# Inverse norms of q and k in two attention layers: a power on GpSimd, or Ln and Exp on ScalarE with a Newton step

## The chip, the cores and the metric

The kernel runs on one core of a Trainium2 chip. The metric is the device time of one execution in microseconds, as the median of the runs. Engines are called PE (TensorE), PEld (its weight loads), DVE (VectorE), ACT (ScalarE), POOL (GpSimd) and SP (SyncE), as in the profile.

## The reference

The input is 16 sequences of 512 tokens with 256 channels. A first part, attention over 16 heads with residual and layer norm, is not touched. Then come two layers, and this is what one of them computes for q, k and v:

```python
h = shift_token(x)                      # second half of the channels from the token before
q, k, v = split(h @ wqkv)               # 8 heads of 64
q = l2norm(q) * qs;  k = l2norm(k) * ksc   # l2norm(t) = t / clip(norm(t), 1e-12)
q, k = rotary_xpos(q, k)
o = local_attention(q, k, v)            # windows of 128 keys and the 128 before, softmax
x = x + o @ wo
h = layernorm(shift_token(x)) * lg + lb
a, g = split(h @ w1 + b1)
x = x + (a * gelu(g)) @ w2 + b2
```

After both layers a residual and a final layer norm are added. All inputs and outputs are float32.

## The kernel before, in words

The first part (`head_attention`) runs first, up to about 1560 us. The rest is `layers`. It works through 32 sequences (16 in layer 1, numbered 0 to 15, and the same 16 in layer 2, numbered 16 to 31), each in 4 tiles of 128 tokens. `T` is the tile's number, `w_` its place in its sequence (0 to 3). Every engine has its own list of instructions, which it carries out strictly in the order written; `one(n, par, r, layer)` writes the four tiles of sequence n. The first four, the last two of layer 1, the first two of layer 2 and the last ones are written out singly, the others run in hardware loops. Engines wait for one another on semaphores.

The work is staggered. While tile T is in attention, the engines project q, k and v of tile T+1, and the feed-forward part works on tile T-4: its hidden values come in three chunks (i = 0, 1, 2) in `hidden` (L1445), ScalarE adds the bias to the gate half of each (`gate`, L1056) and VectorE to the value half (`value`, L1196). `value` waits for `gate` of its chunk. When the gate values of half a sequence (two tiles) are there, ScalarE applies Gelu to all of them in two instructions (L1109, L1110); this is done in the tiles with w_ = 0 and w_ = 2, for sequences n-2 and n-1. VectorE multiplies the value half of the first of the two tiles by it (`gated`, L843 and L845), GpSimd the second. Then PE forms the product with w2 (L1524), which waits for `gated`.

The norms: ScalarE squares q and k of tile T+1 out of PSUM (`squares`), VectorE sums them per head into `ss` (L1163) and clips them into `ssc` (L1167, 128 x 16), GpSimd raises `ssc` to the power -0.5 (`norms`, L959) into `rn`. `rn` is read by `scale_k` on VectorE (L1171), after which PE transposes k (L1474), and in the next tile by the exp bias (L1187) and the exps (L1137).

Within one tile the orders that matter are these. ScalarE: layer norm of T-2, q and k evacuated, gate(T,0), evacuate_hT, oT, exps of half 0, squares(T+1), PT evacuated, Gelu where there is one, gate(T,1), exps of half 1, evacuate_v(T+1), gate(T,2), PT evacuated. VectorE: ..., row_max of half 0, the residual x2, final_stats (in layer 2, w_ = 0 and 2), rot_products(T+1) with ss and ssc, value(T,1), row_max of half 1 (L1184) with the exp bias (L1187), gated, value(T,2), scale_k(T+1), final_norm, layer-norm statistics of T-1, residual xo. GpSimd: rounding rest of hnT, rotate(T+1), norms(T+1), the final rstd (L995), rstd (L1000), its half of gated. PE: ..., hidden(T,1), scores of half 1, times_v, v of T+1, hidden(T,2), the w2 product, transposes of the probabilities of half 1, and then the next tile's transposes of q and k.

Each function of ScalarE needs a table that holds it. [...] Where the program doesn't name a set, the load (ACT_TABLE_LOAD) is put directly in front of the first instruction that needs another one; it carries the line of that instruction.

Of the kernel before, what the change touches and what calls it, by code (L numbers as in the profile page):

```python
# [47 lines left out]
def head_attention(nc, ctx, x_in, w, x_out, consts, W0=None, raw=None):  # L48
# [6 lines left out]


    ident, identr, half = consts["ident"], consts["identr"], consts["minus_half"]
    ones_row, minus_identb = consts["ones_row"], consts["minus_identb"]

    def sb(name, shape, dtype=F32):  # L60
        return ctx.enter_context(nc.sbuf_tensor("a_" + name, shape, dtype))
# [542 lines left out]
def make_constants(nc, ctx):  # L604
    def sb(name, shape, dtype=F32):
        return ctx.enter_context(nc.sbuf_tensor("c_" + name, shape, dtype))

    c = {"ident": sb("ident", [P, P]), "identr": sb("identr", [P, P], F32R),
         "identb": sb("identb", [P, P], BF16), "minus_identb": sb("minus_identb", [P, P], BF16),
         "minus_half": sb("half", [P, 16]), "ones_row": sb("ones", [1, P])}  # L610
    s_i = ctx.enter_context(nc.semaphore("c_identity"))
    with nc.Block() as block:
        @block.gpsimd
        def _(pool):
            nc.gpsimd.memset(c["minus_half"][:], -0.5).then_inc(s_i, 1)
            nc.gpsimd.memset(c["ones_row"][:], 1.0).then_inc(s_i, 1)
            nc.gpsimd.memset(c["ident"][:], 0.0).then_inc(s_i, 1)
            pool.wait_ge(s_i, 3)
            nc.gpsimd.affine_select(out=c["ident"][:], in_=c["ident"][:], compare_op=ALU.not_equal, fill=1.0, base=0,
                                    pattern=[[-1, P]], channel_multiplier=1).then_inc(s_i, 1)  # L620

        @block.vector
        def _(dve):
            dve.wait_ge(s_i, 4)
            nc.vector.tensor_copy(c["identr"][:], c["ident"][:]).then_inc(s_i, 1)
            nc.vector.tensor_copy(c["identb"][:], c["ident"][:]).then_inc(s_i, 1)
            nc.vector.tensor_scalar(c["minus_identb"][:], c["ident"][:], -1.0, None, ALU.mult).then_inc(s_i, 1)
            dve.wait_ge(s_i, 7)
    return c


# [54 lines left out]
def layers(nc, ctx, x_a, x_b, y_out, w, W, raw, consts):  # L686
# [37 lines left out]
    t2 = [sb(f"t2{i}", [P, LHEADS, LDIM]) for i in range(2)]  # L724
    ss = sb("ss", [P, 2 * LHEADS])
    ssc = sb("ssc", [P, 2 * LHEADS])
    rn = [sb(f"rn{i}", [P, 2 * LHEADS]) for i in range(2)]
    qT = sb("qT", [P, 2, PAIRS, P], F32R)
    kT = sb("kT", [P, 2, PAIRS, 2, P], F32R)
# [43 lines left out]
    s_ss = sem("sums_of_squares")  # L773
    s_qr = sem("q_rotated")
    s_ks = sem("k_sum")
    s_rn = sem("norms")
    s_kr = sem("k_rotated")
    s_qkT = sem("qkT")
# [169 lines left out]
    def _(pool):  # L948
# [5 lines left out]
            nc.gpsimd.tensor_tensor(t1[1][:], t1[1][:], t2[1][:], ALU.add).then_inc(s_ks, 1)  # L954

        def norms(t, p):
            pool.wait_ge(s_ss, 2 * t + 2)
            need(pool, s_pr, 2 * t - 2)
            nc.gpsimd.tensor_tensor(rn[p][:], ssc[:], half[:], ALU.pow).then_inc(s_rn, 1)  # L959

        nc.gpsimd.memset(zero_col[:], 0.0).then_inc(s_c, 1)
        for i in range(2):
            nc.gpsimd.memset(hT1[i][:].bitcast(F32), 0.0).then_inc(s_c, 1)
            nc.gpsimd.memset(a_sb[i][:], 1.0).then_inc(s_c, 1)
            nc.gpsimd.memset(mask[i][:], 0.0).then_inc(s_c, 1)
        nc.gpsimd.memset(hs[:], 0.0).then_inc(s_c, 1)
        pool.wait_ge(s_c, 8)
        for i in range(2):

            nc.gpsimd.affine_select(out=mask[i][:, i], in_=mask[i][:, i], compare_op=ALU.is_ge, fill=MASKED, base=0,  # L970
# [39 lines left out]
    def _(act):  # L1010
# [28 lines left out]
        def squares(t):  # L1039
# [3 lines left out]
            act.wait_ge(s_k, t + 1)  # L1043
            nc.scalar.activation(sq[:, 1], X[1][:], ACT.Square).then_inc(s_sq, 1)

        def evacuate_v(t, w_):
            act.wait_ge(s_v, t + 1)
            need(act, s_AV, t - 2)
            nc.scalar.activation(v[:, w_], X[2][:], ACT.Copy).then_inc(s_ve, 1)
# [18 lines left out]

        split_high(0)
        act.wait_ge(s_w, WEIGHTS)  # L1070
        act.wait_ge(s_c, 12)
        evacuate_hT(-1, -1, 3, lambda d: 0)
        squares(0)
        evacuate_v(0, 0)

        def one(n, par, r, layer):
            for w_ in range(TILES):
                T = TILES * n + w_
                p = w_ % 2
                live, feed = tile_exists(T), seq_exists(n - 1)  # L1080
                if tile_exists(T - 2):
                    layernorm(T - 2, p, (w_ - 2) % TILES, par if w_ >= 2 else 1 - par)
                if live:
                    act.wait_ge(s_qkT, 2 * T + 1)
                    nc.scalar.activation(qT[:, HIGH], X[0][:].rearrange("p (b q) -> p b q", q=P), ACT.Copy).then_inc(s_qkTe, 1)
                    act.wait_ge(s_qkT, 2 * T + 2)
                    nc.scalar.activation(kT[:, HIGH, :, p], X[1][:].rearrange("p (b q) -> p b q", q=P), ACT.Copy
                                         ).then_inc(s_qkTe, 1)
                if feed:
                    gate(T, 0, w_, layer)  # L1090
                if tile_exists(T + 1) or tile_exists(T - 2):
                    evacuate_hT(T, n, w_, layer)
                if tile_exists(T - 1):
                    act.wait_ge(s_oT, T)
                    nc.scalar.activation(oT[:], M[:], ACT.Copy).then_inc(s_oTe, 1)
                if live:
                    exps(T, w_, 0)
                if tile_exists(T + 1):
                    squares(T + 1)
                if live:  # L1100
                    act.wait_ge(s_PT, 2 * T + 1)
                    evacuate_PT(w_, 0)
                if w_ % 2 == 0:
                    h, d = (1, 2) if w_ == 0 else (0, 1)
                    m = n - d
                    if seq_exists(m):

                        act.wait_ge(s_Fg, 3 * (TILES * m + 2 * h + 2))
                        nc.scalar.activation(g_sb[h][0:HC, 0:CHUNKS - 1], g_sb[h][0:HC, 0:CHUNKS - 1], ACT.Gelu)  # L1109
                        nc.scalar.activation(g_sb[h][0:LAST, CHUNKS - 1], g_sb[h][0:LAST, CHUNKS - 1], ACT.Gelu  # L1110
                                             ).then_inc(s_ge, 1)
                if feed:
                    gate(T, 1, w_, layer)
                if live:
                    exps(T, w_, 1)
                if tile_exists(T + 1):
                    evacuate_v(T + 1, (w_ + 1) % TILES)
                if feed:
                    gate(T, 2, w_, layer)
                if live:  # L1120
                    act.wait_ge(s_PT, 2 * T + 2)
                    evacuate_PT(w_, 1)
                if split_at(n, w_) is not None:
                    split_high(split_at(n, w_))
                if isinstance(n, int) and n == ALL_SEQS + 1 and w_ == 2:
                    break
# [22 lines left out]
    def _(dve):  # L1149
        def rot_products(t, w_, layer):  # L1150
# [13 lines left out]
                                    ).then_inc(s_ss, 1)  # L1164
            dve.wait_ge(s_ss, 2 * t + 1)
            need(dve, s_rn, t)
            nc.vector.tensor_scalar(ssc[:], ss[:], 1e-24, None, ALU.max).then_inc(s_ss, 1)  # L1167

        def scale_k(t, p):
            dve.wait_ge(s_rn, t + 1)  # L1170
# [40 lines left out]
            nc.vector.tensor_tensor(hT1[1 - p][:, LOW, 0:1], last_col, hT1[1 - p][:, HIGH, 0:1], ALU.subtract  # L1211
                                    ).then_inc(s_hTl, 1)

        dve.wait_ge(s_c, 12)
        split_low(0)
        low_hT(-1, 3)
        dve.wait_ge(s_w, WEIGHTS)
# [116 lines left out]
    def _(pe):  # L1334
# [114 lines left out]
            last.then_inc(s_F, 1)  # L1449

        pe.wait_ge(s_w, WEIGHTS)
        pe.wait_ge(s_c, 12)
        tile_parity["next"] = 0
        transpose_h(-1, -1, 3, 1)
        projection_ready(0, 0)
# [145 lines left out]
```

## Time and profile before

| | |
|---|---|
| time, median of 3 runs | 4568.05 us (4567.26 to 4568.8) |
| the profiled execution | 4568.7 us, its span 4566.8 us |
| mean granted TensorE clock | 0.982 |
| busy: PE, PEld | 4268.7 us (93%), 3555.8 us (78%) |
| busy: DVE, ACT, POOL | 3151.7 us (69%), 2677.8 us (59%), 2373.7 us (52%) |

Times are microseconds unless marked ns. In the rows of stretches the engines stand in the order PE, PEld, DVE, ACT, POOL, with the number of instructions in brackets. A busy share is one of the engine's whole span. "Idle before" is the time in which an engine stood still ahead of an instruction, with the instruction that ended it behind the arrow. Ends of matmuls are modelled, so a product can seem to overlap the next by 0.1 to 0.2 us.

### The profile page before, as it was taken

What the parts mean: (1) busy time and instruction counts of PE and PEld (TensorE: products, weight loads), DVE (VectorE), ACT (ScalarE), POOL (GpSimd) and SP (SyncE); (2) the same over time, 40 slices, a digit from 0 to 9 for tenths busy, and PEclk for the clock granted to TensorE, in tenths of its full rate; (3) what the DMA queues carried; (4) which work ended last, traced back from release to release, by engine and by line L of the source; (5) the groups of instructions that cost most, each with busy time, mean ns of one, the idle gap of its engine ahead of it and who ended that gap; (6) DMA issues with size and microseconds to landing.
All of it is one profiled execution on the core that took longest, in us unless ns stands there. A gap on an engine that the chain in (4) does not pass through costs nothing.

```text
span 4566.8 us, 99388 instructions
## 1 busy us (share of the span) xinstructions
PE 4268.7 (93%) x36868; PEld 3555.8 (78%) x36928; DVE 3151.7 (69%) x5876; ACT 2677.8 (59%) x6240; POOL 2373.7 (52%) x1655
## 2 busy tenths in 40 slices
PE   5999999999999589999999999999999999999998
PEld 3666666666676478888888888888888888888887
DVE  4989898898999655565555555555666666666664
ACT  3544454444544256666766666666666666666664
POOL 4989898898999633333333333333333333333332
PEclk8999999999999899999999999999999999999999
DMA  5443444344443100000000000000000000000000
GB/s 107 68 61 58 64 68 69 60 60 65 67 64 50 44 27 13 13 16 18 16 14 17 20 14 15 18 28 13 20 21 25 18 23 18 26 20 20 21 21 25
DMA packets 175117, 160.11 MB, mean 35 GB/s; under 512 B 22175, under 2 KB 173558, under 8 KB 174582
## 3 DMA queue, kind: packets, MB, share of 16 engines
q1 hardware_dynamic: 174582, 153.04, 18.1%
q8 instruction: 329, 5.39, 0.5%
q14 instruction: 206, 1.69, 0.1%
HBM read 52.31 MB, written 25.17 MB: 17 GB/s over the span
## 4 chain that ended last, share of the span: by engine, by line
PE 46%; DVE 7%; issue 6%; ACT 4%; POOL 2%; SPq 0%; DVEq 0%; DMA 0%; ACTq 0%; POOLq 0%
PE b_X L1374 10%; PE b_F L1445 7%; PE b_M L1419 7%; PE b_M L1497 5%; PE b_F L1524 5%; PE b_S L1399 4%; PE b_S L1408 3%; PE b_M L1488 2%; PE b_S L1390 2%; ACT b_p L1137 1%; PE b_X L1470 1%; PE b_X L1474 1%; POOL b_rn L959 1%; ACT b_hn L1036 1%; DVE b_ss L1163 1%
## 5 line engine op out<-in xcount | busy, mean ns | idle before, releaser
L321 ACT ACTIVATE a_p<-a_S 128x512 f32<-128x512 f32 x1024 | 529.3, 603 | 593.4 <-PE a_S L507 593.4
L373 DVE TENSOR_REDUCE a_nm<-a_S 128x128 fp32r<-128x2048 f32 x256 | 586.3, 2290 | 130.2 <-PE a_S L497 123.6
L1137 ACT ACTIVATE b_p<-b_S,b_nb,b_rn 128x256 f32<-128x256 f32 (+1 forms) x1024 | 536.7, 534 | 230.5 <-DVE b_nb L1187 229.7
L1374 PE MATMUL b_X<-b_wqkv,b_hT 128*128 128x512 f32 x2304 | 648.2, 417 | 3.6 <-DVE b_hT L1211 1.3
L250 POOL TENSOR_TENSOR a_z<-a_p 128x1024 f32<-128x1024 f32 x256 | 604.0, 2360 | 74.4 <-ACT a_p L321 73.1
L1445 PE MATMUL b_F<-b_hnT,b_w 128*114 128x256 f32 (+1 forms) x4608 | 630.6, 286 | 5.7 <-issue 5.7
L1445 PEld LDWEIGHTS b_F<-b_hnT,b_w 128*114 128x114 f32 (+1 forms) x4608 | 575.3, 178 | 18.6 <-issue 5.9
L952 POOL TENSOR_TENSOR b_t<-b_t 128x512 f32<-128x512 f32 x128 | 165.6, 1293 | 792.3 <-DVE b_t L1161 792.3
L1374 PEld LDWEIGHTS b_X<-b_wqkv,b_hT 128*128 128x128 f32 x2304 | 417.3, 190 | 91.4 <-issue 8.0
L1196 DVE TENSOR_SCALAR b_a<-b_F,w_b 114x256 f32<-114x256 f32 (+1 forms) x384 | 183.8, 479 | 432.3 <-ACT b_g L1056 432.1
L258 POOL TENSOR_TENSOR a_p<-a_p,a_zi 128x640 f32<-128x640 f32 x256 | 397.4, 1552 | 98.9 <-DVE a_zi L399 98.5
L1419 PE MATMUL b_M<-b_v,b_PT 128*128 128x64 f32 x3584 | 445.4, 276 | 0.0
L1419 PEld LDWEIGHTS b_M<-b_v,b_PT 128*128 128x128 f32 x3584 | 424.3, 193 | 15.0
L1143 ACT ACTIVATE b_PT<-b_S 128x1024 f32<-128x1024 f32 (+1 forms) x256 | 235.2, 919 | 319.6 <-PE b_S L1408 319.6
L401 DVE TENSOR_TENSOR a_p<-a_p,a_O 128x1408 f32<-128x1408 f32 x256 | 412.2, 1610 | 0.0
L507 PE MATMUL a_S<-a_nm,c_identr 128*128 128x512 f32 x1024 | 313.8, 428 | 95.8 <-DVE a_nm L373 85.1
L959 POOL TENSOR_TENSOR b_rn<-b_ssc,c_half 128x16 f32<-128x16 f32 x128 | 372.7, 2912 | 21.2 <-DVE b_ssc L1167 16.8
L984 POOL TENSOR_TENSOR b_hnT<-b_hnT 128x256 fp32r<-128x256 f32 x128 | 93.8, 733 | 555.5 <-ACT b_hnT L1027 555.5
L507 PEld LDWEIGHTS a_S<-a_nm,c_identr 128*128 128x128 f32 x1024 | 175.0, 191 | 266.1 <-DVE a_nm L373 229.4
L1524 PE MATMUL b_F<-w_w,b_a 114*128 114x256 f32 (+1 forms) x1536 | 361.9, 385 | 15.8 <-DVE b_a L845 14.4
L1000 POOL TENSOR_TENSOR b_rstd<-b_ve,c_half 128x1 f32<-128x1 f32 x128 | 71.0, 555 | 562.7 <-DVE b_ve L1288 562.7
L253 POOL TENSOR_TENSOR a_z<-a_z 128x512 f32<-128x512 f32 x256 | 327.8, 1280 | 23.0 <-POOL a_z L250 5.7
(143 smaller groups left out, 8805.4 us busy)
## 6 DMA issues: line engine op xcount, KB each, us to landing
a_q<-a_parts SPq DMA_DIRECT2D x256, 128.0 KB, 4.9
a_k<-a_parts SPq DMA_DIRECT2D x256, 128.0 KB, 5.0
a_x<-in_x SPq DMA_DIRECT2D x16, 512.0 KB, 4.1
a_xr<-in_x SPq DMA_DIRECT2D x64, 128.0 KB, 5.0
x_after_heads<-a_n SPq DMA_DIRECT2D x64, 128.0 KB, 5.0
b_x<-x_after_heads SPq DMA_DIRECT2D x16, 512.0 KB, 3.9
x_after_layer<-b_xo SPq DMA_DIRECT2D x32, 256.0 KB, 2.2
b_x<-x_after_layer SPq DMA_DIRECT2D x16, 512.0 KB, 3.9
```

The lines of the kernel that those rows point to most:

```text
L250: nc.gpsimd.tensor_tensor(z8[:], e[:, 0:8], e[:, 8:16], ALU.add).then_inc(s_zt, 1)
L258: nc.gpsimd.tensor_tensor(e, e, zinv[u % 2][:].unsqueeze(1).to_broadcast([P, HEADS - DVE_HEADS, P]), ALU.mult).then_inc(s_pp, 1)
L321: nc.scalar.activation(probs[u % NE][:, hs], S[:, hs], ACT.Exp, scale=HDIM ** -0.5).then_inc(s_exp, 1)
L373: nc.vector.tensor_reduce(out=negmax[u % 2][:], in_=S[:].rearrange("p h q -> p q h"), axis=AX.X, op=ALU.max, negate=True).then_inc(s_nm, 1)
L401: nc.vector.tensor_tensor(e, e, ZI.unsqueeze(1).to_broadcast([P, DVE_HEADS, P]), ALU.mult).then_inc(s_p, 1)
L507: nc.tensor.matmul(S[:, 4 * b:4 * b + 4], identr[:], negmax[u % 2][:].unsqueeze(1).to_broadcast([P, 4, P]), start=False, stop=True, skip_g ...
L959: nc.gpsimd.tensor_tensor(rn[p][:], ssc[:], half[:], ALU.pow).then_inc(s_rn, 1)
L1137: last = nc.scalar.activation(probs[hf][:, i, keys(w_)], SB[:, i, keys(w_)], ACT.Exp, bias=nb[hf][:, i:i + 1], scale=rn[w_ % 2][:, h:h + 1 ...
L1374: last = nc.tensor.matmul(X[i][:], hT_of(k, a), wqkv[:, b, k, i * INNER:(i + 1) * INNER], start=(k == 0 and (a, b) == PART_PAIRS[0]), stop ...
L1419: last = nc.tensor.matmul(M[:, h * LDIM:(h + 1) * LDIM], PT[hf][:, i, a * P:(a + 1) * P], v[:, w_ if a == w_ % 2 else w_ - 1, h * LDIM:(h ...
L1445: last = nc.tensor.matmul(F[i % 2][0:size, part], w1[:, a, k, col:col + size], hnT[:, b, k, hf * 2 * P:(hf + 1) * 2 * P], start=(k == 0 an ...
L1524: last = nc.tensor.matmul(F[1][:, t], a_sb[h][0:rows, c, t * P:(t + 1) * P], W[layer(-d)]["w2"][0:rows, c], start=(c == 0), stop=(c == CHU ...
```

## The change

GpSimd's power is replaced by a first estimate from ScalarE, exp(-0.5 ln(ss)), and one Newton step g(1.5 - 0.5 ss g g) in four GpSimd instructions. For that `ssc` now holds -0.5 times the clipped sums. The table set that has both Ln and Exp is named in the program: once before the first tile, and after every pair of Gelus. `guess_norms(T+1)` stands between gate(T,1) and exps of half 1. An unused row of ones is dropped, and the counts of a few waits change with the constants.

```diff
@@ layers
+    ln_ss, guess = sb("ln_ss", [P, 2 * LHEADS]), sb("guess", [P, 2 * LHEADS])
+    newton, three_halves = sb("newton", [P, 2 * LHEADS]), sb("three_halves", [P, 2 * LHEADS])
...
@@ gpsimd
         def norms(t, p):
-            pool.wait_ge(s_ss, 2 * t + 2)
+            pool.wait_ge(s_gs, t + 1)
+            nc.gpsimd.tensor_tensor(newton[:], guess[:], guess[:], ALU.mult).then_inc(s_nw, 1)
+            pool.wait_ge(s_nw, 3 * t + 1)
+            nc.gpsimd.tensor_tensor(newton[:], newton[:], ssc[:], ALU.mult).then_inc(s_nw, 1)
+            pool.wait_ge(s_nw, 3 * t + 2)
+            nc.gpsimd.tensor_tensor(newton[:], newton[:], three_halves[:], ALU.add).then_inc(s_nw, 1)
+            pool.wait_ge(s_nw, 3 * t + 3)
             need(pool, s_pr, 2 * t - 2)
-            nc.gpsimd.tensor_tensor(rn[p][:], ssc[:], half[:], ALU.pow).then_inc(s_rn, 1)
+            nc.gpsimd.tensor_tensor(rn[p][:], newton[:], guess[:], ALU.mult).then_inc(s_rn, 1)
...
+        nc.gpsimd.memset(three_halves[:], 1.5).then_inc(s_c, 1)
@@ scalar
+        def guess_norms(t):
+            act.wait_ge(s_ss, 2 * t + 2)
+            nc.scalar.activation(ln_ss[:], ssc[:], ACT.Ln, scale=-2.0).then_inc(s_ls, 1)
+            act.wait_ge(s_ls, t + 1)
+            need(act, s_rn, t)
+            nc.scalar.activation(guess[:], ln_ss[:], ACT.Exp, scale=-0.5).then_inc(s_gs, 1)
...
         squares(0)
+        nc.scalar.preload_act_table_set("natural_log_exp_and_others")
+        guess_norms(0)
         evacuate_v(0, 0)
...
                         nc.scalar.activation(g_sb[h][0:LAST, CHUNKS - 1], g_sb[h][0:LAST, CHUNKS - 1], ACT.Gelu
                                              ).then_inc(s_ge, 1)
+                        nc.scalar.preload_act_table_set("natural_log_exp_and_others")
                 if feed:
                     gate(T, 1, w_, layer)
+                if tile_exists(T + 1):
+                    guess_norms(T + 1)
                 if live:
                     exps(T, w_, 1)
@@ vector
-            nc.vector.tensor_scalar(ssc[:], ss[:], 1e-24, None, ALU.max).then_inc(s_ss, 1)
+            nc.vector.tensor_scalar(ssc[:], ss[:], 1e-24, -0.5, ALU.max, ALU.mult).then_inc(s_ss, 1)
```

## Rows read from the trace of the kernel before

**Rows 1.** busy time by stretch (start:end, length, engines, PEclk, DMA share, GB/s)

```profile
1900.00:2100.00 200.00, 199.09 (x1441) 175.43 (x1440) 119.86 (x288) 137.98 (x340) 70.81 (x55) 1.00 0.05 16
3300.00:3500.00 200.00, 193.78 (x1381) 169.76 (x1379) 122.51 (x313) 131.37 (x330) 65.52 (x54) 0.99 0.07 20
```

**Rows 2.** the page, chain that ended last, by line, share of span

```profile
PE b_X L1374 10%; PE b_F L1445 7%; PE b_M L1419 7%; PE b_M L1497 5%; PE b_F L1524 5%; PE b_S L1399 4%; PE b_S L1408 3%; PE b_M L1488 2%; PE b_S L1390 2%; ACT b_p L1137 1%; PE b_X L1470 1%; PE b_X L1474 1%; POOL b_rn L959 1%; ACT b_hn L1036 1%; DVE b_ss L1163 1%
```

**Rows 3.** lines L959 (ns) and L1171 (waited for: us, times)

```profile
L959 POOL TENSOR_TENSOR b_rn<-b_ssc,c_half x128: 2909/2912/2919, 1588.8 to 4477.6; 128x16 f32<-128x16 f32 x128
...
  POOL b_rn L959: 9.6, 5
```

**Rows 4.** timeline of ScalarE, layer 1, w_ = 0 (start, length)

```profile
2040.82 0.40 ACT L1110 ACTIVATE b_g<-b_g 112x256 f32<-112x256 f32 x1
2041.13 0.46 ACT L1056 ACTIVATE b_g<-b_F,w_b 114x256 f32<-114x256 f32 x1
2041.60 1.28 ACT L1137 ACT_TABLE_LOAD   x1
2042.93 0.46 ACT L1137 ACTIVATE b_p<-b_S,b_nb,b_rn 128x128 f32<-128x128 f32 x1
```

**Rows 5.** timeline of VectorE, the same tile

```profile
2041.62 0.48 DVE L1196 TENSOR_SCALAR b_a<-b_F,w_b 114x256 f32<-114x256 f32 x1 [0.99 <-ACT b_g L1056]
2042.02 0.68 DVE L1184 TENSOR_REDUCE b_mx<-b_S 128x4 f32<-128x512 f32 x1
2042.73 0.16 DVE L1187 SCALAR_TENSOR_TENSOR b_nb<-b_mx,b_rn 128x4 f32<-128x4 f32 x1
2042.93 0.83 DVE L843 TENSOR_TENSOR b_a<-b_a,b_g 114x640 f32<-114x640 f32 x1
2043.68 0.28 DVE L845 TENSOR_TENSOR b_a<-b_a,b_g 112x128 f32<-112x128 f32 x1
```

**Rows 6.** timeline of PE, the same tile

```profile
2044.09 2.85 PE L1524 MATMUL b_F<-w_w,b_a 114*128 114x256 f32 x12
```

**Rows 7.** timelines of three other kinds of gelu tile

```profile
1999.44 0.28 DVE L845 TENSOR_TENSOR b_a<-b_a,b_g 112x128 f32<-112x128 f32 x1
...
1999.87 2.85 PE L1524 MATMUL b_F<-w_w,b_a 114*128 114x256 f32 x12
...
2899.42 0.28 DVE L845 TENSOR_TENSOR b_a<-b_a,b_g 112x128 f32<-112x128 f32 x1
...
2900.00 2.76 PE L1524 MATMUL b_F<-w_w,b_a 114*128 114x256 f32 x12
...
3315.44 0.46 ACT L1056 ACTIVATE b_g<-b_F,w_b 114x256 f32<-114x256 f32 x1
...
3316.44 0.47 DVE L1196 TENSOR_SCALAR b_a<-b_F,w_b 114x256 f32<-114x256 f32 x1
...
3318.49 0.28 DVE L845 TENSOR_TENSOR b_a<-b_a,b_g 112x128 f32<-112x128 f32 x1
...
3318.90 2.85 PE L1524 MATMUL b_F<-w_w,b_a 114*128 114x256 f32 x12 [0.58 <-DVE b_a L845]
```

**Rows 8.** line L1137, its table loads (ns)

```profile
L1137 ACT ACT_TABLE_LOAD  x61: 1283/1283/1283, 1729.5 to 4477.9; - x61
```

**Rows 9.** timeline of ScalarE: a one-column Copy; exps, ordinary tile

```profile
2007.08 0.19 ACT L1020 ACTIVATE b_hT<-b_X 128x1 fp32r<-128x1 f32 x1
...
2019.68 0.56 ACT L1137 ACTIVATE b_p<-b_S,b_nb,b_rn 128x256 f32<-128x256 f32 x1 [2.36 <-DVE b_nb L1187]
```

**Rows 10.** timeline of GpSimd: 256 and 512 columns

```profile
2008.75 0.73 POOL L984 TENSOR_TENSOR b_hnT<-b_hnT 128x256 fp32r<-128x256 f32 x1 [2.40 <-ACT b_hnT L1027]
...
2016.61 1.27 POOL L954 TENSOR_TENSOR b_t<-b_t 128x512 f32<-128x512 f32 x1
```

**Rows 11.** timelines of VectorE and PE, the drain

```profile
4534.75 1.62 DVE L845 TENSOR_TENSOR b_a<-b_a,b_g 112x128 f32<-112x128 f32 x1
...
4536.43 4.55 PE L1524 MATMUL b_F<-w_w,b_a 114*128 114x256 f32 x12 [2.78 <-DVE b_a L845]
```

More of the change, by code:

```diff
@@ L57, in head_attention @@
     ident, identr, half = consts["ident"], consts["identr"], consts["minus_half"]
-    ones_row, minus_identb = consts["ones_row"], consts["minus_identb"]
+    minus_identb = consts["minus_identb"]
     def sb(name, shape, dtype=F32):
@@ L609, in make_constants @@
          "identb": sb("identb", [P, P], BF16), "minus_identb": sb("minus_identb", [P, P], BF16),
-         "minus_half": sb("half", [P, 16]), "ones_row": sb("ones", [1, P])}
+         "minus_half": sb("half", [P, 16])}
     s_i = ctx.enter_context(nc.semaphore("c_identity"))
@@ L615, in _ @@
             nc.gpsimd.memset(c["minus_half"][:], -0.5).then_inc(s_i, 1)
-            nc.gpsimd.memset(c["ones_row"][:], 1.0).then_inc(s_i, 1)
             nc.gpsimd.memset(c["ident"][:], 0.0).then_inc(s_i, 1)
-            pool.wait_ge(s_i, 3)
+            pool.wait_ge(s_i, 2)
             nc.gpsimd.affine_select(out=c["ident"][:], in_=c["ident"][:], compare_op=ALU.not_equal, fill=1.0, base=0,
@@ L623, in _ @@
         def _(dve):
-            dve.wait_ge(s_i, 4)
+            dve.wait_ge(s_i, 3)
             nc.vector.tensor_copy(c["identr"][:], c["ident"][:]).then_inc(s_i, 1)
@@ L627, in _ @@
             nc.vector.tensor_scalar(c["minus_identb"][:], c["ident"][:], -1.0, None, ALU.mult).then_inc(s_i, 1)
-            dve.wait_ge(s_i, 7)
+            dve.wait_ge(s_i, 6)
     return c
@@ L775, in layers @@
     s_ks = sem("k_sum")
+    s_ls = sem("ln_squares")
+    s_gs = sem("norms_guessed")
+    s_nw = sem("newton_step")
     s_rn = sem("norms")
@@ L966, in _ @@
         nc.gpsimd.memset(hs[:], 0.0).then_inc(s_c, 1)
-        pool.wait_ge(s_c, 8)
+        pool.wait_ge(s_c, 9)
         for i in range(2):
@@ L1070, in _ @@
         act.wait_ge(s_w, WEIGHTS)
-        act.wait_ge(s_c, 12)
+        act.wait_ge(s_c, 13)
         evacuate_hT(-1, -1, 3, lambda d: 0)
         squares(0)
+        nc.scalar.preload_act_table_set("natural_log_exp_and_others")
+        guess_norms(0)
         evacuate_v(0, 0)
@@ L1212, in low_hT @@
                                     ).then_inc(s_hTl, 1)
-        dve.wait_ge(s_c, 12)
+        dve.wait_ge(s_c, 13)
         split_low(0)
@@ L1451, in _ @@
         pe.wait_ge(s_w, WEIGHTS)
-        pe.wait_ge(s_c, 12)
+        pe.wait_ge(s_c, 13)
         tile_parity["next"] = 0
```

## The prediction

> **What bounds the kernel now.** I read the busy time by stretch first (is there an engine with no room?), then the chain and the waits around the power (does anyone wait for the norms?), and last the timelines of single tiles (what comes level with PE?).
>
> The change touches only the layers, after about 1590 us. There PE works 199.09 of 200 us in layer 1 and 193.78 of 200 in layer 2, POOL about 70 [rows 1]. So time that PE loses is lost for good, and time that GpSimd saves counts only where PE waits for it.
>
> It hardly does. The chain gives the power (L959) 1% [rows 2], but the instruction that reads the norms, the scaling of k (L1171), sat idle for them 5 times in 128 tiles, 9.6 us in all [rows 3]. Elsewhere the norms are there before anyone asks. The shares of the chain are inferred; the idle time is what I go by.
>
> What does bind is found in the tiles with a gelu (T with w_ = 0 or 2). There ScalarE does: table load, two Gelus, gate(T,1) (L1056), table load, exps. In the tile shown the Gelus end at 2040.82+0.40 = 2041.22, the gate starts at 2041.13 (back-to-back operations overlap by 0.09), and only then comes the load for Exp, 1.28 us, ending at 2042.88 [rows 4]. VectorE waits for that gate and starts value(T,1) 0.03 us after it; behind it in its queue stand row_max, the exp bias, and gated, whose last part ends at 2043.96 [rows 5]. PE starts the w2 product at 2044.09, 0.13 us later [rows 6]. Where PE is seen to stand idle for L845, the product also starts 0.13 us after it (3318.77 to 3318.90, rows 7), so 0.13 is the latency of that wait and the slack here is nil. The chain gate, value, row_max, bias, gated, w2 product is thus already level with PE, in a stage where PE has no room.
>
> **The change part by part.**
>
> 1. *The table load moves ahead of the gate.* The number of loads in live tiles doesn't change: one before the Gelus, one after. Before, the second stood behind gate(T,1) and in front of exps, where ScalarE would have waited for the bias anyway: load and bias end within 0.01 us of each other, at 2042.88 and 2042.89 [rows 4, 5]. Now it is issued right behind the second Gelu, ahead of the gate. The gate then starts at 2041.22 + 1.28 + 0.01 = 2042.51 instead of 2041.13: 1.38 us later. Queued behind it: value(T,1), row_max, bias and gated on VectorE, and with them the w2 product; exps, evacuate_v and gate(T,2) on ScalarE, value(T,2), scale_k and the layer-norm statistics after those. All move by about the same amount, so PE stalls once per such tile and finds the others no later than itself. There are 61 such tiles, as many as loads in front of Exp [rows 8]: sequences 1 to 31 with w_ = 2, sequences 2 to 31 with w_ = 0. By kind (layer 2's final_stats runs from sequence 18 on):
>  - layer 1, w_ = 0, 16 tiles, slack nil: 16 x 1.38 = 22.1 us.
>  - layer 1, w_ = 2, 17 tiles. L845 ends at 1999.72 and the product starts at 1999.87: 0.15, less the latency 0.13, leaves 0.02 to 0.06 in the 10 looped ones. In the 7 written out singly the distance is 0.30 (2899.70 to 2900.00, rows 7); I take 0.25 of it as slack. 10 x 1.35 + 7 x 1.13 = 21.4.
>  - layer 2, w_ = 2, 14 tiles (12 looped): 12 x 1.35 + 2 x 1.13 = 18.5.
>  - layer 2, w_ = 0, 14 tiles: final_stats holds VectorE, value(T,1) starts at 3316.44 though the gate ended at 3315.44 + 0.46 = 3315.90 [rows 7], so 0.5 us of the delay is covered (I take 0.4 in two of them): 12 x 0.88 + 2 x 0.98 = 12.5.
>  Sum: 74.5 us. Nothing hides it, because the wait that it lengthens is PE's.
>
> The Trainium skill (ScalarE: Activation LUTs, "What ACT_TABLE_LOAD costs") has every switch at 1283 ns for the load and some 1380 ns of drain. The load's length agrees with rows 8 (1283 ns); the drain does not show in rows 4, where the exps start 0.05 us after the load. By the page's sum the gate would be 2.8 us late in each of the 61 tiles: that is rival E.
>
> 2. *Ln and Exp on ScalarE* (guess_norms, between gate(T,1) and exps). No row shows them at 128x16. A Copy of 128x1 takes 0.19 us [rows 9], which is the lower end; an Exp of 128x128 takes 0.46 [rows 4], the upper. I take 0.20, the nearest in columns, with 0.1 for the two waits: 0.5 us for both, 1.1 at most. They wait for ssc, which VectorE writes before value(T,1), row_max and the bias that exps wait for. From the gate's end to the exps are 0.03+0.40+0.68+0.03+0.16+0.04 = 1.34 us even in the short tile [rows 4, 5]; in an ordinary tile ScalarE idles 2.36 us there [rows 9]. Cost nothing; without that cover, 0.5 us for each of 128 tiles.
>
> 3. *GpSimd: four small products and sums for one power.* Removed: 2.91 us a tile [rows 3]. Added: 128x256 takes 0.73 and 128x512 1.27 us [rows 10], so 2.1 ns a column and 0.22 us at 16 columns. With a wait of 0.1 each, 4 x 0.32 = 1.3 us; at most 4 x 0.73 + 0.4 = 3.3, at least 0.9. Guess and step together take 1.8 where the power took 2.9. Behind them in the queue are frstd, rstd and gated's half, none of which had waited for the power. In ordinary tiles the norms come earlier and nobody takes them earlier: 0. In a gelu tile they start 0.5 us after a gate that is itself late: 2042.97 + 0.5 + 1.3 = 2044.8, before even the delayed gated ends (2043.96 + 1.38); scale_k stands behind that and value(T,2), so the norms are still early. Gain: only where L1171 waited. The first power starts at 1588.8 [rows 3] and PE has nothing else to do then, gain about 1.1. The four others sit where PE waits for exps anyway: 0.1 each. Together -1.5 us.
>
> 4. *GpSimd and VectorE side by side.* In the tiles with w_ = 0 the last small GpSimd operation may fall on gated (L843, 0.83 us beside the power, rows 5). The nearest row of two such operations together is the L845 of 1.62 us instead of 0.28 in the drain [rows 11]. The bounds are 0 and +1.34 for each of 30 tiles (+40); the power next to L843 cost nothing and a 16-column operation is short, so I take 0 and keep +10 in the range.
>
> 5. *ssc with a second operator, the new constants, the missing ones row.* Same instruction, same size; memsets before the stage starts: 0, at most 1 us once.
>
> 6. *The drain.* Sequence 32 has no exps, so there no second load stood before; now each Gelu has one behind it, and the next Gelu needs its own. At (32, w_ = 2) that is two loads, 2.57 us, ahead of the gate; final_stats on VectorE covers an estimated 0.3 of it, and PE idles behind L845 already, 2.78 us [rows 11]: +2.3. The others hide behind PE or final_stats. Bounds 0 and +5.
>
> Sum: 74.5 - 1.5 + 2.3 = +75.3 on the profiled execution's 4568.7 us (span 4566.8): 4644.0. The median of the runs is 0.65 below it: **4643 us**, 1.6% slower.
>
> **The rivals.**
>
> *A: the load is hidden after all.* If the load ahead of the gate were placed where Exp is (or PE had room I don't see), the w2 products stay where they are and only part 3's gain is left: 4568.05 - 1.5 = 4567. For it: the loads of before stand directly ahead of their function. Against: rows 4 to 7 leave 0 to 0.25 us of room for 1.38.
>
> *B: the norms matter more than the waits say; faster.* If the chain's 1% were true, the power's 46 us are on the path, and 1.1 of each 2.9 us goes: -17 us. With A's hiding this ends at 4568 - 17 = 4551, faster. It decides if L1171's idle time is misread. Against it: rows 3. With the gate's delay it would be 4626, which is within the range.
>
> *C: the set that serves both isn't kept.* If Ln and Exp each called their own set, an ordinary tile would get two more loads, 2.57 us, plus 0.4, in a gap of 2.36 (+0.6 for 67 tiles) and a gelu tile at least one more before exps (+0.8 to 1.3 for 61): 4643 + 40 + 65 = 4748. The Trainium skill (same page, "Table sets: the hidden batching unit") says that one set holds both, so one load serves them; no row of before shows it.
>
> *D: half of it comes back.* PE idles 6.2 us of 200 in layer 2 [rows 1]; if the shift fed itself into those idle places, up to 0.6 us of each of the 28 tiles there would return: 4643 - 17 = 4626.
>
> *E: ScalarE stands still behind a load.* If another 1.38 us went by before the gate, it would be 61 x 1.38 = 84 us more: 4727. Against it: 0.05 us from load to exps in rows 4, with a bias that ended in the same moment. It is the skill's drain (the section named in part 1).
>
> **How the numbers follow.** Forecast 0.77, D 0.07, A 0.05, B 0.03 (faster only in its pure form), C 0.04, E 0.02, something lost beyond the range 0.02. This kernel's runs tell 0.2% (9 us) from no change. Slower: 0.77+0.07+0.04+0.02+0.02 = 0.92; same 0.05; faster 0.03. The range takes in D and B with the gate's delay below, less a few us for gelu tiles that have more room than those shown, and above it the contention of part 4 and 5 us of drain: 4612 to 4664.
>
> **What would show it.** In the changed profile: L1056 behind a Gelu starts 1.29 us after the Gelu's end, with a load between; the w2 product gets an idle time <- L845 of 0.9 to 1.4 us in some 61 tiles, some 75 us in all (before there are few such waits); PE's busy time stays; the load counts stay near 64 and 64. Ln and Exp at 0.2 us each, with exps still released by the bias; L1171 no longer waits for rn beyond the first tiles; GpSimd's busy time falls by 128 x (2.9-0.9) = 260 us with no gain. I am wrong if the w2 product waits no longer than before, if loads turn up in ordinary tiles, or if exps wait for GpSimd or for Ln.

## The result, and the profile after

| | before | after |
|---|---|---|
| time, median of 4 runs side by side | 4568.43 us (4567.26 to 4577.63) | 4663.48 us (4656.82 to 4670.61) |
| the profiled execution: time, span | 4568.7, 4566.8 us | 4658.6, 4656.8 us |
| mean granted TensorE clock | 0.982 | 0.983 |

The change makes the kernel slower: ratio 1.0206, 95% interval 1.0194 to 1.0218, about 94 us. The forecast was 4643 us with a range of 4612 to 4664. The measured median lies 0.5 us inside the upper end of that range. The two profiled executions are 90.0 us apart in span; the accounting below is made of these.

The page's line of busy times, of the changed kernel (us, share of the span, instructions):

```profile
PE 4287.7 (92%) x36928; PEld 3557.0 (76%) x36928; DVE 3154.2 (68%) x5876; ACT 2744.3 (59%) x6502; POOL 2131.3 (46%) x2039
```

GpSimd has 242 us less to do and the kernel is 90 us longer. What PE waited for in the layers, first after, then before (us in total, times, longest):

```profile
PE b_F L1547 <- DVE b_a L849: 88.6, 64, 3.9
PE b_X L1379 <- ACT b_hn L1047: 29.8, 33, 6.5
```

```profile
PE b_X L1356 <- ACT b_hn L1036: 24.8, 38, 6.5
...
PE b_F L1524 <- DVE b_a L845: 14.4, 17, 3.5
```

One line moved much: the w2 product (L1547, before L1524) waits for `gated` 64 times instead of 17, and 88.6 us instead of 14.4: +74.2 us. The same tile as [rows 4 to 6], on ScalarE, VectorE, GpSimd and PE of the changed kernel (start, length; the last bracket is idle time and its releaser):

```profile
2054.06 0.40 ACT L1130 ACTIVATE b_g<-b_g 112x256 f32<-112x256 f32 x1
2054.48 1.28 ACT L1132 ACT_TABLE_LOAD   x1
2055.78 0.47 ACT L1074 ACTIVATE b_g<-b_F,w_b 114x256 f32<-114x256 f32 x1
2056.15 0.21 ACT L1059 ACTIVATE b_ln_ss<-b_ssc 128x16 f32<-128x16 f32 x1
2056.39 0.22 ACT L1062 ACTIVATE b_guess<-b_ln_ss 128x16 f32<-128x16 f32 x1
2057.60 0.46 ACT L1160 ACTIVATE b_p<-b_S,b_nb,b_rn 128x128 f32<-128x128 f32 x1 [0.99 <-DVE b_nb L1210]
```

```profile
2056.28 0.48 DVE L1219 TENSOR_SCALAR b_a<-b_F,w_b 114x256 f32<-114x256 f32 x1 [2.43 <-ACT b_g L1074]
2056.68 0.68 DVE L1207 TENSOR_REDUCE b_mx<-b_S 128x4 f32<-128x512 f32 x1
2057.40 0.16 DVE L1210 SCALAR_TENSOR_TENSOR b_nb<-b_mx,b_rn 128x4 f32<-128x4 f32 x1
2057.60 0.83 DVE L847 TENSOR_TENSOR b_a<-b_a,b_g 114x640 f32<-114x640 f32 x1
2058.34 0.31 DVE L849 TENSOR_TENSOR b_a<-b_a,b_g 112x128 f32<-112x128 f32 x1
```

```profile
2056.68 0.21 POOL L962 TENSOR_TENSOR b_newton<-b_guess 128x16 f32<-128x16 f32 x1 [2.86 <-ACT b_guess L1062]
...
2057.28 0.22 POOL L966 TENSOR_TENSOR b_newton<-b_newton,b_three_halves 128x16 f32<-128x16 f32 x1
2057.65 0.85 POOL L969 TENSOR_TENSOR b_rn<-b_newton,b_guess 128x16 f32<-128x16 f32 x1 [0.16 <-POOL b_newton L966]
```

```profile
2055.70 1.56 PE L1468 MATMUL b_F<-b_hnT,b_w 128*114 128x256 f32 x12
2058.78 2.86 PE L1547 MATMUL b_F<-w_w,b_a 114*128 114x256 f32 x12 [1.51 <-DVE b_a L849]
```

Read them as a relay. The second Gelu ends at 2054.46, the load takes ScalarE to 2055.76, and the gate starts at 2055.78 where it stood 0.09 us ahead of the Gelu's end before. `value` follows the gate's start by 0.50 us (before 0.49), the product follows `value` by 2.50 us (before 2.47): every leg has its old length, and the baton is late by the load alone. PE ended its other work at 2057.26 and stands for 1.51 us. Behind the gate ScalarE has 0.99 us to spare before its exps, so Ln and Exp cost nothing there.

### The profile page after: what moved, and what is told of

Its sections match the earlier page's. It is cut to its first block, busy times and chain, and to the rows that moved or that the text cites. A ratio compares the mean times of both kernels' runs of the same rounds, so it can differ in the third digit from the quotient of the medians.

```text
span 4656.8 us, 100507 instructions
## 1 busy us (share of the span) xinstructions
PE 4287.7 (92%) x36928; PEld 3557.0 (76%) x36928; DVE 3154.2 (68%) x5876; ACT 2744.3 (59%) x6502; POOL 2131.3 (46%) x2039
## 3 DMA queue, kind: packets, MB, share of 16 engines
q14 instruction: 213, 1.74, 0.1%
## 4 chain that ended last, share of the span: by engine, by line
PE 36%; issue 14%; ACT 7%; DVE 4%; POOL 4%; POOLq 0%; SPq 0%; DMA 0%; DVEq 0%; ACTq 0%
PE b_X L1397 8%; PE b_M L1442 5%; PE b_F L1468 5%; PE b_M L1520 4%; PE b_F L1547 4%; PE b_S L1431 3%; PE b_S L1422 3%; PE b_M L1511 1%; ACT L1129 1%; ACT L1132 1%; PE b_S L1413 1%; ACT b_p L1160 1%; DVE b_mx L1207 1%; ACT b_g L1074 1%; POOL b_t L956 1%
## 5 line engine op out<-in xcount | busy, mean ns | idle before, releaser
L1547 PE MATMUL b_F<-w_w,b_a 114*128 114x256 f32 (+1 forms) x1536 | 363.6, 386 | 89.2 <-DVE b_a L849 88.6
L1547 PEld LDWEIGHTS b_F<-w_w,b_a 114*128 114x128 f32 (+1 forms) x1536 | 284.6, 192 | 138.0 <-issue 71.3
```

The costliest lines, as they stand in the source:

```text
L1547: last = nc.tensor.matmul(F[1][:, t], a_sb[h][0:rows, c, t * P:(t + 1) * P], W[layer(-d)]["w2"][0:rows, c], start=(c == 0), stop=(c == CHU ...
```

## The experiments

Ratios are to the kernel before, run on the same chip in the same series, with a 95% interval. "Step" is by how much a w2 product falls further behind the same product of the kernel before, in the profiles; all steps together give the difference of the spans.

**1. The load alone, without the new norms** (before_load_ahead).

```diff
 (kernel before, behind the second Gelu)
+                        nc.scalar.preload_act_table_set("exp_and_others")
```

> The kernel before, power and all, with one addition: the load of Exp's table is named right behind the second Gelu, so that it runs ahead of gate(T,1). Theory L: it loses what the change lost in these tiles, 16 x 1.45 + 31 x 1.35 + 14 x 0.96 = 78.5 us and some 2 in the drain: 4568 + 80 = 4648, range 4640 to 4660. Rival N: 4568, since no norm is touched. Rival H: the layers start at 1561.8 as before, because no constant is touched; if they start late here too, it is the run and not the kernel.

Measured: 4652.8 us, ratio 1.0186 (1.0169 to 1.0203). PE's wait for `gated`:

```profile
PE b_F L1525 <- DVE b_a L845: 88.0, 64, 3.9
```

With power where it was, and this one line of the change, the 88 us are there. The steps by kind of tile are those of the changed kernel (layer 1, w_ = 0: 1.43; w_ = 2 looped 1.40, written singly 1.18; layer 2, w_ = 0: 0.93 us; in the changed kernel 1.45, 1.40, 1.18 and 0.95).

**2. The changed kernel with its load behind the gate** (load_behind_gate).

```diff
 (kernel after)
-                        nc.scalar.preload_act_table_set("natural_log_exp_and_others")
                 if feed:
                     gate(T, 1, w_, layer)
+                if w_ % 2 == 0 and seq_exists(n - (2 if w_ == 0 else 1)):
+                    nc.scalar.preload_act_table_set("natural_log_exp_and_others")
```

> The changed kernel, with the table load after the Gelus put back behind gate(T,1), ahead of Ln. Theory L (the load ahead of the gate is the whole loss, 61 tiles of about 1.4 us): the w2 product waits for gated as rarely as before, and the kernel comes back to about 4577 us where before is 4568: 2 us of drain, and some 9 us because in the 30 tiles with w_ = 0 load, Ln and Exp end 0.45 us after the exp bias, so that gate(T,2) and the layer norm of the tile come that much later. Range 4566 to 4584. Rival N (Ln, Exp and the four GpSimd operations cost the time by themselves): it stays above 4620. Rival H (part of the loss, about 4 us, comes from the constants that moved, since the attention part ended 4.1 us later in the changed kernel's profile): the first instruction of the layers on ScalarE starts at 1565.9 here too, not at 1561.8.

Measured: 4591.66 us, ratio 1.0057 (1.004 to 1.0073). The wait for `gated` is gone, but the kernel stays 21 us behind that of before, above the range I had written. What stands where (PE's wait for `gated`; then ScalarE at the load; then ScalarE and PE at the back-edge of layer 1's loop):

```profile
PE b_F L1548 <- DVE b_a L849: 15.2, 17, 3.6
```

```profile
2045.54 1.28 ACT L1135 ACT_TABLE_LOAD   x1
2046.83 0.22 ACT L1059 ACTIVATE b_ln_ss<-b_ssc 128x16 f32<-128x16 f32 x1
2047.08 0.22 ACT L1062 ACTIVATE b_guess<-b_ln_ss 128x16 f32<-128x16 f32 x1
2047.21 0.44 ACT L1161 ACTIVATE b_p<-b_S,b_nb,b_rn 128x128 f32<-128x128 f32 x1
```

```profile
2123.04 0.49 ACT L1047 ACTIVATE b_hn<-b_x,b_shift,b_rstd 128x128 f32<-128x128 f32 x1 [1.89 <-DVE b_shift L1258]
2125.09 0.49 ACT L1047 ACTIVATE b_hn<-b_hs,b_shift,b_rstd 128x128 f32<-128x128 f32 x1 [1.56 <-issue]
```

```profile
2125.63 0.44 PE L1380 MATMUL b_X<-c_ident,b_hn 128*128 128x128 f32 x2 [1.96 <-ACT b_hn L1047]
2125.91 3.21 PE L1443 MATMUL b_M<-b_v,b_PT 128*128 128x64 f32 x16
```

Two smaller costs come to light. One had been hidden by the load ahead of the gate. In this order Ln and Exp stand between the load, which ends level with the bias, and the exps, which start 0.38 us later for it: 0.28 us a step in layer 1's first tiles (w_ = 0), 16 x 0.28 = 4.5 us. The other is in the changed kernel too (part 2 below): at each of the four back-edges of layer 1's loop ScalarE stands 1.6 to 1.8 us for nothing that the trace names, between the two hn instructions. In the one shown PE then waits 1.96 us, and after that its 16 small matmuls take 3.21 us, where they take 1.90 at the full clock. The granted clock in these stretches was (window, length, busy times by engine, PEclk):

```profile
2123.00:2126.00 3.00, 1.04 (x10) 0.80 (x8) 0.00 (x0) 1.41 (x4) 0.00 (x0) 1.00 0.02 8
2126.00:2129.00 3.00, 3.00 (x18) 3.00 (x17) 1.68 (x3) 2.70 (x10) 0.22 (x1) 0.54 0.00 0
```

The four back-edges gave steps of 4.38, 1.74, 4.66 and 1.84 us, 12.6 together. The two large ones are those where the small matmuls slowed down (3.21 and 3.19 us), after waits of PE of 1.96 and 2.46 us; after waits of 1.99 and 2.30 us at the two others they kept 1.90. With the 4.5 these make 17 of the 21 us. Of the rest, 3.0 us stood before the first gelu tile (2.7 of them before the layers, see below) and 1.1 in the drain.

**3. Norms that cost next to nothing** (cheap_norms). The power is replaced by a subtraction, so rn is no inverse norm.

```diff
 (kernel before)
-            nc.gpsimd.tensor_tensor(rn[p][:], ssc[:], half[:], ALU.pow).then_inc(s_rn, 1)
+            nc.gpsimd.tensor_tensor(rn[p][:], ssc[:], half[:], ALU.subtract).then_inc(s_rn, 1)
```

> The kernel before with GpSimd's power replaced by one subtraction of the same shape, so that rn holds no inverse norm (that part of the computation is left out): 0.22 us instead of 2.91 in every tile. It is the most that any cheaper norm can bring. Theory L (nobody waits for the norms but the first tiles): 4566 us where before is 4568, -3 to 0. Rival B (the chain's 1% for the power is real): -17 to -46 us, 4522 to 4551.

Measured: 4567.24 us, ratio 0.9995 (0.9985 to 1.0004). GpSimd's busy time fell from 2373.7 to 2028.1 us for nothing. VectorE's wait for the norms, which was 9.6 us in 5 times [rows 3]:

```profile
DVE b_t L1171 <- POOL b_rn L959: 0.3, 1, 0.3
```

So the whole cost of the power was below 0.2%. Rival B, by which the norms lie on the path, falls.

**4. Two loads ahead of the gate** (two_loads_ahead).

```diff
 (kernel after, behind the second Gelu)
+                        nc.scalar.preload_act_table_set("exp_and_others")
                         nc.scalar.preload_act_table_set("natural_log_exp_and_others")
```

> The changed kernel with a second table load (Exp's own set, then the set of both) ahead of gate(T,1). Theory L: each microsecond ahead of the gate is paid 61 times, now without slack: +61 x 1.28 = 78 us above the changed kernel, and 1 to 3 in the drain: ratio to before 1.037 to 1.040, about 4742 us if the changed kernel is at 4663. Rival: if part of the loss in the changed kernel is not the gate's delay but something that a second load doesn't add to (norms, code, constants), it is still +78 for this step, but load_behind_gate then stays well above before; if the two loads run beside each other or with a standstill of 1.38 us each, the step is near 0 or near 160.

Measured: 4806.18 us, ratio 1.053 (1.0513 to 1.0548); span 146.9 us above the changed kernel's. I expected +78. PE's wait for `gated` and its busy time:

```profile
PE b_F L1548 <- DVE b_a L849: 169.0, 64, 5.2
```

```profile
PE 4363.9 (91%) x36868; PEld 3631.4 (76%) x36928; DVE 3154.5 (66%) x5876; ACT 2822.4 (59%) x6566; POOL 2130.6 (44%) x2039
```

I had written that a standstill with each load would bring the step near 160, and 147 is not far from that. But the two loads follow each other without one:

```profile
1967.54 1.28 ACT L1132 ACT_TABLE_LOAD   x1
1968.83 1.28 ACT L1133 ACT_TABLE_LOAD   x1
1970.12 0.47 ACT L1074 ACTIVATE b_g<-b_F,w_b 114x256 f32<-114x256 f32 x1
```

The wait grew by 80.4 us, 78.5 of it in the 61 tiles, as the theory has it, and 1.9 in the drain, which has three more such loads. But PE was also busy for 76.2 us longer with the same matmuls. The products of two gelu tiles, and the granted clock behind the second (window, its length, the five engines' busy times, and then PEclk):

```profile
1926.15 2.86 PE L1548 MATMUL b_F<-w_w,b_a 114*128 114x256 f32 x12 [2.31 <-DVE b_a L849]
...
1973.15 4.54 PE L1548 MATMUL b_F<-w_w,b_a 114*128 114x256 f32 x12 [2.83 <-DVE b_a L849]
```

```profile
1973.00:1975.00 2.00, 1.85 (x5) 1.56 (x6) 0.32 (x2) 1.66 (x6) 0.00 (x0) 0.63 0.00 0
1975.00:1978.00 3.00, 3.00 (x13) 2.42 (x13) 1.71 (x8) 0.00 (x0) 1.23 (x2) 0.68 0.01 3
1978.00:1980.00 2.00, 2.00 (x20) 2.00 (x18) 0.37 (x2) 1.83 (x5) 1.25 (x2) 1.00 0.01 4
```

After standing 2.83 us PE ran at a lower granted clock, 0.63 over the next 2 us (a mean of the 2.4 and the 1.2 GHz level), and the product took 4.54 us instead of 2.86. After 2.31 us in the tile shown it did not, and after the changed kernel's 1.51 us neither. Over the 61 tiles, all 22 products behind a stand of 2.79 us or more took 3.98 us or more; of the 39 behind 2.29 to 2.62 us, 27 were slow and 12 kept 2.85 or 2.86. A second load thus costs nearly twice its length (146.9 us for 61 tiles). The stands of ScalarE at layer 1's back-edges are absent in this kernel, though it has Ln and Exp.

**5. The gate of chunk 1 ahead of the Gelus, in the kernel before** (gate_first) **and after** (gate_first_after). This was to be the better version.

```diff
+                if feed:
+                    gate(T, 1, w_, layer)
                 if w_ % 2 == 0:
                     h, d = (1, 2) if w_ == 0 else (0, 1)
...
-                if feed:
-                    gate(T, 1, w_, layer)
```

> The kernel before, with ScalarE's gate of chunk 1 moved ahead of the Gelu block instead of behind it. Theory (what ends last at a Gelu tile is the path gate, VectorE's value and product, down-projection on TensorE): the path gets shorter by the Gelu block, so the 14.4 us that TensorE waits for the gated product (17 times in layers' loops) go, and some of the 24.8 us that it waits for ScalarE's hn; against that the Gelu itself is later by one gate (0.3 to 0.5 us) at its own reader, which is not near. Ratio 0.994 to 0.998 (about -10 to -25 us). Rival (the product of the chunk before, or the maxima of VectorE, end the wait just as late): ratio 0.999 to 1.001.

> The changed kernel with the same move: ScalarE's gate of chunk 1 stands ahead of the Gelu block and so ahead of the load that was put behind the Gelu. Theory (the 88.6 us of waits for the gated product are the load of 1.28 us in the gate's path and nothing else): the waits go back to below 15 us, and the ratio to the kernel before is 0.996 to 1.004. Rival (the load costs by standing ahead of the second half's exponentials, or the norms' new chain costs): the ratio stays above 1.01.

Measured: 4591.67 us, ratio 1.0044 (1.0027 to 1.0061), and 4625.94 us, ratio 1.0125 (1.0106 to 1.0143). In the kernel before the move loses 20 us instead of gaining 10 to 25. The waits of PE and, below, ScalarE in a gelu tile of gate_first:

```profile
PE b_X L1356 <- ACT b_hn L1036: 34.3, 45, 6.5
...
PE b_F L1524 <- DVE b_a L845: 17.1, 17, 3.5
PE b_X L1474 <- DVE b_t L1171: 8.5, 19, 4.5
```

```profile
2045.86 0.47 ACT L1056 ACTIVATE b_g<-b_F,w_b 114x256 f32<-114x256 f32 x1 [0.76 <-PE b_F L1445]
2046.35 1.28 ACT L1111 ACT_TABLE_LOAD   x1
```

The 14.4 us that PE waited for `gated` did not hang on the gate, and they are still there: 14 of the 17 waits are the w_ = 0 tiles of layer 2 (0.24 to 0.59 us each), where `value` starts behind final_stats [rows 7], and three are in the drain. In the looped w_ = 0 tiles of layer 1 the move does bring the w2 product 0.2 to 0.5 us sooner, but the next product then falls back by 1.1. What the move did is make ScalarE wait for the hidden product (0.76 us here) before the Gelus instead of doing the Gelus meanwhile, so that Gelu, load, exps and all behind them came later: in this tile PE then stood 0.18 us for the scaled k, 0.51 for hn and 0.24 for o_n, where before only the last was there. In gate_first_after the wait for `gated` is

```profile
PE b_F L1547 <- DVE b_a L849: 18.5, 17, 4.4
```

so 70 of the 88.6 us went by taking the load off the gate's path, as in experiment 2, and the wait for hn rose to 51.4 us in their place. My upper figure for this run (1.004) was missed. The profile has two things for it: the product behind each w_ = 0 tile of layer 1 falls back by 1.2 to 1.5 us (0.9 to 1.1 in gate_first), and ScalarE stands 1.5 us at the four back-edges of layer 1, which in gate_first it does not; the steps there are 5.65, 1.28, 1.21 and 1.34 us.

**6. Two small operations on ScalarE, without and with Ln's wait** (two_more_copies, waiting_copies).

```diff
 (kernel before, behind gate(T, 1); the two tiles `spare` are new)
+                if tile_exists(T + 1):
+                    act.wait_ge(s_ss, 2 * (T + 1) + 2)     # waiting_copies alone
+                    need(act, s_rn, T + 1)                 # waiting_copies alone
+                    for i in range(2):
+                        nc.scalar.activation(spare[i][:], half[:], ACT.Copy)
```

> The kernel before, with two copies of 128x16 on ScalarE into tiles that nobody reads, in each tile with a successor, where the changed kernel has its Ln and Exp; power, and the loads where they were. Theory (the two operations as such are hidden, and the 1.6 us for which ScalarE stands between the two hn instructions at the loop's back-edges of layer 1 comes from the number of its instructions in the loop's body): +0 to +10 us, ratio 1.000 to 1.002, and the stand between the two hn instructions is in the trace, 4 times. Rival (the stand has to do with the Ln and Exp's waits or with where the load stands): ratio 0.999 to 1.001 and no such stand.

> The kernel before, with the two copies of 128x16 on ScalarE of the kernel two_more_copies (they read a constant and write tiles that nobody reads), and ahead of them the waits that the changed kernel has ahead of its Ln: for VectorE's clamped sums of the next tile, and for GpSimd's norm of this one; power, and the loads where they were. Theory (the stand of 1.6 us between the two hn instructions at the back-edges of layer 1, and the 0.28 us of a first tile, both come with this wait standing in ScalarE's order ahead of the second half's exponentials): the stand is in the trace 4 times, and the ratio is 1.002 to 1.005, near the kernel with the load behind the gate. Rival (they come with Ln and Exp themselves, or with where the load stands): no stand, ratio 0.999 to 1.001.

Measured: ratio 1.0004 (0.9994 to 1.0014) and 1.0043 (1.0027 to 1.006). The two operations as such are nearly hidden: no stand at the back-edges, steps of 0.12 to 0.20 in the w_ = 0 tiles of layer 1, 2.6 us together. So the number of instructions alone was not the cause of the stand. With the waits, the ratio rises to near that of experiment 2, with steps of 0.12 to 0.21 in the w_ = 0 tiles of layer 1, 0.4 to 0.5 in those of layer 2, and 0.62 to 1.14 at the four back-edges of layer 1. There ScalarE stands again, but at another place and for half as long:

```profile
2124.69 0.60 ACT L1088 ACTIVATE b_kT<-b_X 128x512 fp32r<-128x512 f32 x1 [0.73 <-issue]
```

The theory is right in a small part: waits in that place bring a stand at the back-edge, but not the 1.6 us one between the hn instructions, and they add nothing to the steps of the w_ = 0 tiles of layer 1. The ratio fell into the range that I had written by luck: the steps of 0.4 to 0.5 in layer 2 make some 6 us of it, and experiment 2 has none there.

**7. Ln and Exp behind the exps** (norms_after_exps), in the kernel of experiment 2.

```diff
-                if tile_exists(T + 1):
-                    guess_norms(T + 1)
                 if live:
                     exps(T, w_, 1)
                 if tile_exists(T + 1):
+                    guess_norms(T + 1)
                     evacuate_v(T + 1, (w_ + 1) % TILES)
```

> The changed kernel with its load behind the gate of chunk 1, and Ln and Exp of the next tile behind the second half's exponentials instead of ahead of them. Theory (what is left of the cost once the load is off the gate's path is the wait of Ln for the clamped sums, ahead of the exponentials): the 0.28 us of each first tile goes, with or without the stand at the back-edges, and the ratio to the kernel before is 0.999 to 1.003, below that of the load behind the gate (1.0057). Rival (the norms are then late for k's rotation and the transposes behind it, since Ln, Exp and four Newton steps of 0.3 us start 2 us later): ratio above 1.005, with longer waits of TensorE for VectorE's scaled k than 4.8 us.

Measured: 4626.39 us, ratio 1.0122 (1.0105 to 1.0139). The range that I had written for the theory was missed, and the 0.28 us did not go: the steps behind the w_ = 0 tiles of layer 1 are 0.31 to 0.43. The rival was right in direction, but only for the start: the norms come late in the first five tiles, before 1681 us, and nowhere else, and the first w2 product is 9.1 us late. VectorE's wait for the norms, and PE's for the scaled k and for hn:

```profile
DVE b_t L1195 <- POOL b_rn L969: 16.9, 5, 3.9
```

```profile
PE b_X L1380 <- ACT b_hn L1047: 43.3, 40, 5.7
...
PE b_X L1498 <- DVE b_t L1195: 9.0, 7, 4.0
```

The back-edges of layer 1 cost 4.5 to 6.1 us each here, 23 us of the 60 by which the spans differ. In layer 2 the products fall back by 0.3 to 0.5 us for every gelu tile, 12 us together; why, was not tested. Of the orders tried for the new norms, that of experiment 2 is the cheapest, and none reaches the kernel before.

## Why the prediction was right, point by point

The direction, the mechanism and its place were as forecast; the total was 15 us (profiled) to 20 us (medians) too low. That the median still lies in the range, by 0.5 us, is in part luck: the room above the forecast was meant for contention and for the drain, and neither used it. It was used up by larger steps, by the stands at the back-edges, by a later start of the layers, and by differences between single executions. Against the 90.0 us of the two spans:

| term | forecast | measured |
|---|---|---|
| 1. load ahead of the gate | 74.5 | 78.5 by steps, 74.2 by PE's waits |
| 2. Ln and Exp | 0 | 0 in this order; back-edges of layer 1: +6.4 |
| 3. norms earlier | -1.5 | -1.0 |
| 4. GpSimd beside VectorE | 0 | 0 |
| 5. constants, start of the layers | 0, at most 1 | +1.9 |
| 6. drain | +2.3 | +1.3 |
| the part before the layers (unchanged) | 0 | +4.1 |
| tiles ahead of the first Gelu | 0 | -1.2 |

*Part 1.* By kind of tile the steps were 1.45, 1.40 (1.18 where written singly), 1.40 (1.18) and 0.95 (1.06 to 1.13) us; forecast were 1.38, 1.35 (1.13), 1.35 (1.13) and 0.88 (0.98). All are larger by some 0.06 us, which over 61 tiles is near 4 us: the gate used to overlap the Gelu by 0.09 and now follows the load after 0.02 (I had 1.38 for 1.28 + 0.09 + 0.01), and the legs behind it are 0.01 to 0.03 longer. Experiments 1 and 2 show this term from both sides: the load alone brings it, the load behind the gate takes it away. Rivals A and D fall with it. The steps of the w_ = 0 tiles at the five back-edges of layer 2 scatter (1.17, -0.01, 2.15, 0.22 and 0.07 us), as they do in other profiles (-1.93 to 1.80 in experiment 2); together they are 1.2 us below five plain ones, which is all that layer 2 can have given back.

*Part 2.* Ln and Exp take 0.21 and 0.22 us; I had 0.20. They cost nothing where they stand, but for a reason that the change itself makes: with the load ahead of the gate, ScalarE is idle between gate and exps. That cover was forecast at 1.34 us and measured 1.35 (2056.25 to 2057.60 above). It holds for this order alone: with the load in its old place it fills the gap, and the steps are 0.28 us in the w_ = 0 tiles. What I missed is the stand at the loop's back-edges of layer 1: steps of 2.89, 3.12, 3.04 and 3.24 us where a plain tile has 1.45, 4 x 1.6 = 6.4 us. The rows, with the same instruction of before behind them (there no stand):

```profile
2134.72 0.49 ACT L1047 ACTIVATE b_hn<-b_x,b_shift,b_rstd 128x128 f32<-128x128 f32 x1 [1.80 <-DVE b_shift L1257]
2136.85 0.49 ACT L1047 ACTIVATE b_hn<-b_hs,b_shift,b_rstd 128x128 f32<-128x128 f32 x1 [1.63 <-issue]
```

```profile
2118.88 0.49 ACT L1036 ACTIVATE b_hn<-b_x,b_shift,b_rstd 128x128 f32<-128x128 f32 x1 [2.07 <-DVE b_shift L1234]
2119.28 0.48 ACT L1036 ACTIVATE b_hn<-b_hs,b_shift,b_rstd 128x128 f32<-128x128 f32 x1
```

It does not come from the load alone (experiment 1 has steps of 1.28 to 1.51 there) nor from two more operations (experiment 6). The stand of 1.5 to 1.8 us is in four of the five kernels with Ln and Exp, at all four back-edges; the fifth of them, experiment 4, has none. Of the six kernels without Ln and Exp only the one with the waits (experiment 6) has a stand, the shorter one. Its cause is open: the trace names no releaser, and it moved and shrank when only the waits were added.

*Part 3.* The four Newton operations take 0.21 to 0.22 us, 0.30 apart (forecast 0.32). VectorE's wait for the norms fell from 9.6 us to 2.8 in 3 times. In the first tile the k transposes came 1.0 us sooner behind those of q (forecast 1.1); from the others nothing is seen. Experiment 3 caps what any norm could win.

*Part 4.* The contention appeared, and on the other engine: in 30 of 128 tiles the last Newton operation takes 0.81 to 0.88 us beside `gated` (2057.65 above, 0.22 elsewhere), while `gated` keeps its 0.83 us [rows 5]. These are the 30 in which the two overlap. Nobody waits for that norm. The +10 of the range was not needed for it.

*Part 5.* I gave at most 1 us for the constants. From ScalarE's first instruction of the layers to its first evacuation of hT 17.9 us went by before and 19.8 in the changed kernel. In the four other kernels with the new norms it is 19.8 to 20.0, in the five others without them 17.6 to 18.0, so these 1.9 us do belong to the change. PE waits there for the DMA of x: it starts 6.8 us after that DMA's issue before, and 8.7 us after it now. Why it comes later no run shows.

*Part 6.* At (32, w_ = 2) PE's wait grew from 2.78 [rows 11] to 3.89 us:

```profile
4625.85 0.29 DVE L849 TENSOR_TENSOR b_a<-b_a,b_g 112x128 f32<-112x128 f32 x1
```

The second part of `gated`, which had taken 1.62 us [rows 11], took 0.29. That gave back 1.3 of the two loads' 2.57 us. Over the whole drain the kernel falls back by 1.3 us.

*Before the layers.* The first part's own work is not changed, yet the first ScalarE instruction of the layers came at 1565.9 us, 4.1 later than in the profile of before (1561.8). In the nine experiments' profiles it came at 1560.2 to 1567.1 us, with the new norms at 1562.0 to 1567.1 and without them at 1560.2 to 1567.1, so this difference of single executions is not the change's. The 1.2 us that come back between the first tile's k transposes and the first gelu tile I cannot place.

*Rivals C and E.* There are 64 loads in front of the Gelus and 64 behind them (before: 62 and 61), none in ordinary tiles, so C falls. E, by which ScalarE stands still behind a load, falls with the 0.02 us between the load's end and the gate. The Trainium skill (ScalarE: Activation LUTs, "What ACT_TABLE_LOAD costs") has 1380 ns of drain beside each load; no such time shows here, and two loads in a row (experiment 4) added 78.5 us of waits for 61 loads, 1.29 us each, which is the load's own length. The Trainium skill (same page, "Table sets: the hidden batching unit") has one set with both Ln and Exp, and the trace agrees: in ordinary tiles both run without a load.

## What to carry to other kernels

A table load put ahead by name is still an instruction in its engine's queue: put it behind whatever another engine is waiting for, even if the function that needs it comes last. Before moving work off a busy-looking engine, read who waits for its result; here 128 powers of 2.9 us each were worth less than 0.2%. And when one large cost is taken out, measure again: the slack that it made had been hiding a smaller one (Ln and Exp, 0.28 us a tile).

## What the runs showed of the hardware

- TensorE's clock: after the 2.83 us stand of experiment 4 the granted clock fell to 0.63 and the product took 4.54 us instead of 2.86. The same was seen after 1.96 us at a back-edge (0.54; 3.21 us instead of 1.90), but not after 2.31 us in another tile, so the length of the stand alone does not decide it. In experiment 4 all 22 products behind stands of 2.79 us or more were slow, and 27 of the 39 behind 2.29 to 2.62 us.
- ScalarE stood 1.5 to 1.8 us at each back-edge of layer 1's loop with no releaser in the trace in four kernels, 0.7 to 0.8 us at another instruction in a fifth, and not at all in the six others, which differ from these by small edits in the loop.
- A GpSimd operation of 128x16 takes 0.22 us, and 0.81 to 0.88 us when it falls on VectorE's 114x640 product, which itself is not lengthened. The power of the same shape took 2912 ns [rows 3].
